# Routing stage of a mixture-of-experts layer: transposes ahead of products, row scales in pairs, a running sum by doubling, the tile map moved forward

## The chip, the cores and the metric

The kernel runs on one core of a Trainium2 chip. The metric is the device time of one execution in microseconds (us), taken as the median over runs. The core has five engines that run side by side and meet at semaphores: PE (TensorE, matrix products), DVE (VectorE), ACT (ScalarE), POOL (GpSimd) and SP (SyncE, which here only starts transfers). Transfers run on 16 DMA engines.

## The reference, cut to what matters

Two layers, each a recurrence ("cond") followed by a feed-forward part ("ffn"), added to x. The first ffn is attention and a mixture of experts over 1024 tokens of width 256; the change lies in its routing:

```
x = o @ wo + residual                       # end of attention
h = rmsnorm(x, ff_ln_w)
ht = h.reshape(-1, 256)                     # 1024 tokens
logits = ht @ gate_w                        # 8 experts
top_vals, top_idx = top_k(logits, 2)
gates = softmax(top_vals)
for e in range(8):
    we = sum(gates * (top_idx == e), axis=-1)
    ye = silu(ht @ w1[e]) * (ht @ w3[e]) @ w2[e]
    out = out + we[:, None] * ye
```

The second layer's recurrence and its ffn in 8-bit rounding follow; the work on their inputs runs beside the experts.

## The kernel before, in words

Every engine has one program, written out by hand; the order of the code is the order of the queue, and an instruction that waits holds back all that stands behind it on its engine. The stages around the change are these.

**Attention** ends with the output projection of the last four of the eight row tiles of 128 tokens (banks pb and pw). DVE adds the residual (`residual`, L1202, semaphore `x1a_done`, 3 and 4 for the last two pairs of tiles). Tiles 0 to 3 had theirs in the middle of attention, and their second norm is finished inside the attention steps.

**Second norm and gate.** For a tile ACT sums the squares (`squares_of_tile`, L838), POOL makes the reciprocal root of the sum (`rstd`, L1557 and L1558), DVE scales the rows into h2 (`second_norm`, L1212). SP stores each h2 tile to h2_dram. PE transposes the tile (2 instructions, L481), ACT copies the transpose out of the bank (`copy_h2T`, L862), PE multiplies it by gate_w (2 instructions of 8 columns, L485). `route(i)` holds a tile's transposes and products one behind the other.

**Choice of experts and slots.** DVE takes the two largest logits, makes 0/1 masks M1, M2 and their sum MK (L1241 to L1259). PE counts along the tokens of a tile (L529) and over each whole tile (L530). DVE adds up the tile totals one after the other (L1270, eight dependent additions of 128x8), rounds each expert's count up to whole tiles of 128 slots (L1272 to L1277), gives every token its two slots (L1279 to L1284), makes one-hot tables (L1295 to L1300), from which PE gets the token number of every slot (L536, bank pw, `ids_done`), and DVE writes these as integers (row_ids, L1309, `ids_ready`). The tile map (which expert each of the 23 tiles of slots belongs to, L1304 to L1307) and the end tile of each expert (L1311) also come from here; `tmap_ready` releases PE, ACT and SP.

`link(...)` lets an instruction raise a semaphore and DVE wait for it before the next one.

**Experts.** POOL gathers token rows for a tile of slots from h2_dram (L1640), four tiles ahead, then prepares the second layer's recurrence (L1572, L282), whose exponentials ACT makes (L717, L723) before its first silu (L932). PE transposes the rows (L575), multiplies by w1 and w3 (L583), and so on for 23 tiles. SP loads the experts' weights (`load_expert`; experts 1 and 2 start behind the stores of h2). POOL gathers the rows of the second ffn's weights (L1626) before the token rows.

**Last stage.** The second ffn, eight row tiles: products in `gate_up` (L659), transposes L670, products L680.

Of the kernel before, what the change touches and what calls it, by code (L numbers as in the profile page):

```python
# [13 lines left out]
P = 128  # L14
B, S, D = 4, 256, 256
TT = S // P
NT = B * TT
# [45 lines left out]
def build(nc, t, out):  # L63
    ctx = ExitStack()
    with ctx:
# [56 lines left out]
        def recurrence_buffers(base):  # L122
# [81 lines left out]
        lg, M1, M2, MK, tots, pos, prod = (rt[:, k, :] for k in range(7))  # L204
        m8 = rt[:, 7, :]
        i8 = rt[:, 8, :].bitcast(U32)
        car = rt[:, 9:11, :].rearrange("p a n -> p (a n)")[:, 0:(NT + 1) * NE]
# [36 lines left out]
            "hot_ready ids_done ids_ready identb_ready "  # L244
# [120 lines left out]
        def _(pe):  # L365
# [107 lines left out]
            def route(i):  # L473
# [8 lines left out]
                last.then_inc(s["h2T_done"], 1)  # L482
                pe.wait_ge(s["h2T_copied"], i + 1)
# [38 lines left out]
            pe.wait_ge(s["zeros_ready"], 1)  # L522
# [3 lines left out]
            for i in range(NT):  # L526
                route(i)
# [168 lines left out]
        def _(act):  # L696
# [168 lines left out]
            for i in range(4, NT):  # L865
                squares_of_tile(i)
            for i in range(1, NT):
                copy_h2T(i)
# [153 lines left out]
        def _(dve):  # L1022
# [187 lines left out]
            def second_norm(i):  # L1210
                dve.wait_ge(s["rstd2_ready"], i + 1)
# [48 lines left out]
            V.memset(car[:, 0:NE], 0.0).then_inc(s["d_ready"], 1)  # L1260
# [28 lines left out]
            link(V.tensor_copy(placef[:, :, :], place[:, :, :]))  # L1289
# [7 lines left out]
            for k in range(2):  # L1297
                V.tensor_tensor(hot_tile[:, k * NT:(k + 1) * NT], hot_tile[:, k * NT:(k + 1) * NT], over(token_id, MT), ALU.mult)
# [243 lines left out]
        def _(pool):  # L1542
# [197 lines left out]
```

## Time and profile before

| what | value |
|---|---|
| runs of the kernel before | 684.99, 678.54 and 681.04 us, median 681.04 |
| profiled execution | 683.2 us, of it the span of the trace 681.4 us |
| busy in the span | PE 507.7 us (75%), DVE 512.9 (75%), ACT 356.4 (52%), POOL 264.3 (39%) |
| mean granted TensorE clock | 0.916 of full speed |

The span runs from the first to the last instruction; the profiled execution's own time is 1.8 us more. No engine is busy throughout: the kernel is a line of stages with different limits, so what an edit is worth is read in its stage.

### The profile page before, as it was taken

Reading aid. Unit: us, or ns where it says so; the run is one execution under the profiler, and the core shown is the slowest. Engines: PE = TensorE matmul, PEld = TensorE weight load, DVE = VectorE, ACT = ScalarE, POOL = GpSimd, SP = SyncE. Lnnn points to the kernel's source line nnn. Section 1 sums busy time; section 2 is a strip of 40 time slices with the busy share of each in tenths; the row PEclk is TensorE's granted clock in tenths of the full one; section 3 lists DMA queues with packets and bytes.
Section 4 is the critical chain, followed back from the end, with each engine's and each line's share of the span. In section 5 each row is a group of like instructions: output and inputs, shape, how many; then the busy total and the mean of one; then the engine's idle time right before and its main releaser. Section 6 shows DMA issues by size and latency. Waiting matters only on the chain.

```text
span 681.4 us, 9298 instructions
## 1 busy us (share of the span) xinstructions
PE 507.7 (75%) x3018; PEld 345.2 (51%) x3018; DVE 512.9 (75%) x970; ACT 356.4 (52%) x758; POOL 264.3 (39%) x219
## 2 busy tenths in 40 slices
PE   2011296789999999997189989999999998046763
PEld 1001132468888788875145646566656665023442
DVE  4999875788888889872729779879798786379672
ACT  3236145677777778762034554635734554256452
POOL 3465024744444456415180683633350500530001
PEclk9999998799999999997579989999999999667685
DMA  8200003040000000004811942351443110210000
GB/s 269 99 0 0 0 1 123 5 158 1 2 1 1 1 1 25 9 1 141 257 39 28 313 85 44 120 148 29 173 144 117 25 23 16 79 53 8 16 16 24
DMA packets 28362, 44.23 MB, mean 65 GB/s; under 512 B 4795, under 2 KB 21435, under 8 KB 28059
## 3 DMA queue, kind: packets, MB, share of 16 engines
q1 hardware_dynamic: 20843, 31.43, 14.2%
q0 software_dynamic: 3072, 8.14, 5.0%
q10 hardware_dynamic: 4400, 4.06, 1.7%
q8 instruction: 25, 0.41, 0.3%
q14 instruction: 22, 0.18, 0.1%
HBM read 38.51 MB, written 5.12 MB: 64 GB/s over the span
## 4 chain that ended last, share of the span: by engine, by line
PE 52%; DVE 24%; ACT 8%; issue 7%; POOL 5%; DMA 1%; SPq 0%; ACTq 0%; DVEq 0%; POOLq 0%
PE pb L407 10%; PE pw L407 8%; PE pb L583 7%; PE sc L446 6%; PE sc L583 5%; PE po L407 4%; PE pt L457 3%; PE sc L659 2%; PE pb L659 2%; DVE areg L1077 2%; DVE areg L1063 2%; DVE areg L1061 2%; PE pt L592 1%; POOL breg L1626 1%; DVE areg L1410 1%
## 5 line engine op out<-in xcount | busy, mean ns | idle before, releaser
L583 PE MATMUL pb<-wreg,areg 128*128 x184 | 85.1, 606 | 0.8 <-ACT areg L898 0.8
L407 PE MATMUL pb<-areg,wreg 128*128 128x512 f16 x240 | 63.5, 404 | 14.3 <-ACT breg L800 9.0
L1598 POOL TENSOR_TENSOR breg<-breg,con 128x512 f32<-128x512 f32 x32 | 40.6, 1270 | 83.5 <-ACT breg L800 83.5
L407 PE MATMUL pw<-areg 128*128 128x256 f16 x406 | 59.5, 283 | 7.7 <-DVE areg L1418 7.7
L583 PE MATMUL sc<-wreg,areg 128*128 x184 | 63.2, 486 | 0.0
L808 ACT ACTIVATE breg<-breg,mx 128x128 f32<-128x128 f32 (+1 forms) x128 | 56.6, 445 | 1.6 <-DVE mx L1185 1.6
L583 PEld LDWEIGHTS pb<-wreg,areg 128*128 128x128 f32 x184 | 33.9, 195 | 36.3 <-issue 36.1
L407 PEld LDWEIGHTS pw<-areg 128*128 128x128 f16 x406 | 40.7, 101 | 18.3 <-DVE areg L1418 11.2
L446 PE MATMUL sc<-areg,breg 128*128 128x128 f32 (+1 forms) x256 | 47.7, 330 | 0.4 <-DVE mx L1185 0.4
L1640 POOL DMA_INDIRECT areg<-h_dram,row_ids x23 | 31.5, 1371 | 40.6 <-PE po L575 22.4
L1593 POOL TENSOR_TENSOR breg<-breg 128x512 f32<-128x512 f32 x32 | 44.4, 1388 | 4.5
L407 PEld LDWEIGHTS pb<-areg,wreg 128*128 128x128 f16 x240 | 22.7, 101 | 43.1 <-ACT breg L800 12.4
L817 ACT CAST breg<-pt 128x768 f16<-128x768 f32 x32 | 25.5, 798 | 34.9 <-PE pt L457 34.9
L446 PEld LDWEIGHTS sc<-areg,breg 128*128 128x128 f32 x256 | 38.8, 193 | 7.2 <-issue 1.5
L583 PEld LDWEIGHTS sc<-wreg,areg 128*128 128x128 f32 x184 | 33.2, 190 | 18.3
L1134 DVE TENSOR_TENSOR breg<-pb,con 128x512 f32<-128x512 f32 x40 | 27.6, 689 | 18.4 <-PE pb L407 15.9
L1185 DVE CUSTOM_DVE_ANT_0 breg<-sc,con 128x128 f32<-128x128 f32 (+1 forms) x128 | 38.1, 353 | 3.7 <-issue 1.2
L932 ACT ACTIVATE areg<-pb 128x512 f32<-128x512 f32 x23 | 13.8, 599 | 51.7 <-PE pb L583 51.6
L910 ACT ACTIVATE areg<-wreg 128x1792 f16 x23 | 39.6, 1724 | 0.0
L384 PE MATMUL sc<-con,areg 128*128 128x128 f32 x16 | 4.5, 435 | 46.0 <-DVE areg L1080 46.0
L1404 DVE TENSOR_TENSOR areg<-areg,pb 128x512 f32<-128x512 f32 x23 | 15.7, 683 | 29.5 <-ACT areg L932 20.6
L407 PE MATMUL po<-breg,areg 128*128 128x256 f16 (+1 forms) x384 | 36.9, 246 | 0.3 <-DVE areg L1196 0.3
(239 smaller groups left out, 1285.8 us busy)
## 6 DMA issues: line engine op xcount, KB each, us to landing
wreg<-in_L_ffn_w SPq DMA_DIRECT2D x24, 896.0 KB, 7.9
ys_dram<-areg ACTq DMA_DIRECT2D x23, 128.0 KB, 1.8
wreg<-in_L_ffn_wq SPq DMA_DIRECT2D x1, 2048.0 KB, 9.3
wreg<-in_L_ffn_wo SPq DMA_DIRECT2D x1, 2048.0 KB, 8.2
areg<-in_fside_BxSxS ACTq DMA_DIRECT2D x4, 256.0 KB, 5.7
x_in<-in_x SPq DMA_DIRECT2D x4, 256.0 KB, 5.4
h_dram<-areg SPq DMA_DIRECT2D x8, 128.0 KB, 1.7
out_dram<-areg SPq DMA_DIRECT2D x8, 128.0 KB, 1.7
```

The lines of the kernel that those rows point to most:

```text
L407: last = nc.tensor.matmul(bank, w(a), m(b), start=first and k == 0, stop=final and k == 2)
L446: last = nc.tensor.matmul(sc2[:, b, o:o + w], qr[:, buf, b * S + qb * P:b * S + (qb + 1) * P], kT[:, kv, pair * PAIR + b * S:pair * PAIR + ...
L583: last = nc.tensor.matmul(bank, xsT[:, parity, c * P:(c + 1) * P], wreg[:, bass.ds(base + (m * C + c) * FF + lo, w)], start=c == 0, stop=c ...
L659: last = nc.tensor.matmul(bank, qxT[:, c, :], w_fold[m][:, a, c, k * IH:(k + 1) * IH], start=c == 0 and a == 0, stop=c == C - 1 and a == 1)
L808: last = nc.scalar.activation(pr[:, parity, b, o:o + w], pr[:, parity, b, o:o + w], ACT.Exp, bias=mx[:, parity, k:k + 1], scale=-1.0, accu ...
L817: nc.scalar.copy(pT[:, parity, 0], pt2[:, :, 0:BLK]).then_inc(s["pThi_done"], 1)
L910: nc.scalar.activation(w2s[parity][0].rearrange("p c n -> p (c n)"), wreg[:, bass.ds((e % RING) * WEXP + 2 * C * FF, FC * D)], ACT.Copy, s ...
L1134: V.tensor_tensor(t1[:, parity, :].rearrange("p (b n) -> p b n", b=2), bank[:, :].rearrange("p (b n) -> p b n", b=2), rope_cos.rearrange(" ...
L1185: last = V.tensor_tensor_reduce(out=pr[:, parity, b, o:o + w], in0=sc2[:, b, o:o + w], in1=mask[:, o:o + w], scale=-SCALE, scalar=3e38, op ...
L1593: G.tensor_tensor(dst, t1[:, parity, :], t2[:, parity, :], ALU.add).then_inc(s["radd_done"], 1)
L1598: G.tensor_tensor(t2[:, parity, :].rearrange("p (b n) -> p b n", b=2), t2[:, parity, :].rearrange("p (b n) -> p b n", b=2), rope_sin.rearr ...
L1640: G.indirect_dma_start(out=xs[n % 4], out_offset=None, in_=h2_dram[:, :], in_offset=bass.IndirectOffsetOnAxis(ap=row_ids[:, n:n + 1], axis ...
```

## The change

- PE: `route` is cut in two. The transposes of tile i+1 now stand ahead of the products of tile i.
- ACT: behind the copy of tile 0 come the squares of tiles 4 and 5, then the copy of tile 1, then the squares of tiles 6 and 7. Before, all four squares came ahead of the copy of tile 1.
- POOL: the reciprocal roots are made for two tiles by one pair of instructions, and wait for the squares of both. POOL also clears a new buffer `prefix` at the start of the program.
- DVE: the running sum over tiles is made in three additions of 72 columns, each of the buffer and itself shifted by 8, 16 and 32 columns. The addition that gives `pos` moves ahead of the rounding of the counts, without a wait of its own. The two masked products and the two sums behind them lose the wait between them. The comparison of the tile map (cmp) moves behind the slots, its sum behind `placef`, and the map (tmi) and the ends (endi) ahead of hot_place. `tmap_ready` is raised behind identb, at the end.

```diff
-        lg, M1, M2, MK, tots, pos, prod = (rt[:, k, :] for k in range(7))
+        prefix = sb("prefix", [P, 4, NT * NE // 2 + (NT + 1) * NE])
+        sums_from = NT * NE // 2
+        lg, M1, M2, MK, prod2, pos, prod = (rt[:, k, :] for k in range(7))
-        car = rt[:, 9:11, :].rearrange("p a n -> p (a n)")[:, 0:(NT + 1) * NE]
+        car = prefix[:, 3, sums_from:]
...
-            for i in range(NT):
-                route(i)
+            for i in range(NT + 1):
+                if i < NT:
+                    route_transposes(i)
+                if i >= 1:
+                    route_products(i - 1)
...
             copy_h2T(0)
-            for i in range(4, NT):
-                squares_of_tile(i)
-            for i in range(1, NT):
+            squares_of_tile(4)
+            squares_of_tile(5)
+            copy_h2T(1)
+            squares_of_tile(6)
+            squares_of_tile(7)
+            for i in range(2, NT):
                 copy_h2T(i)
...
             def second_norm(i):
-                dve.wait_ge(s["rstd2_ready"], i + 1)
+                dve.wait_ge(s["rstd2_ready"], i // 2 + 1)
...
-            V.memset(car[:, 0:NE], 0.0).then_inc(s["d_ready"], 1)
+            dve.sem_inc(s["d_ready"], 1)
...
+            def before_by(x, n):
+                return x[:, sums_from - n:sums_from - n + (NT + 1) * NE]
+
+            dve.wait_ge(s["zeros_ready"], 2)
             dve.wait_ge(s["rank_done"], 1)
-            link(V.tensor_copy(tots, po[:, 256:256 + NT * NE]))
-            for i in range(NT):
-                link(V.tensor_tensor(car[:, (i + 1) * NE:(i + 2) * NE], car[:, i * NE:(i + 1) * NE], tots[:, i * NE:(i + 1) * NE], ALU.add))
+            link(V.tensor_copy(prefix[:, 0, sums_from + NE:], po[:, 256:256 + NT * NE]))
+            for k in range(3):
+                src = prefix[:, k]
+                link(V.tensor_tensor(before_by(prefix[:, k + 1], 0), before_by(src, 0), before_by(src, NE << k), ALU.add))
+
+            V.tensor_tensor(pos, po[:, 128:128 + NT * NE], car[:, 0:NT * NE], ALU.add)
...
-            link(V.tensor_tensor(pos, po[:, 128:128 + NT * NE], car[:, 0:NT * NE], ALU.add))
-            for k, M in enumerate((M1, M2)):
-                link(V.tensor_tensor(prod, pos, M, ALU.mult))
-                link(V.tensor_reduce(out=slotf[:, k, :], in_=te(prod), axis=AX.X, op=ALU.add))
-            link(V.tensor_copy(sloti[:, :, :], slotf[:, :, :]))
+            V.tensor_tensor(prod, pos, M1, ALU.mult)
+            link(V.tensor_tensor(prod2, pos, M2, ALU.mult))
+            V.tensor_reduce(out=slotf[:, 0, :], in_=te(prod), axis=AX.X, op=ALU.add)
+            link(V.tensor_reduce(out=slotf[:, 1, :], in_=te(prod2), axis=AX.X, op=ALU.add))
+            V.tensor_copy(sloti[:, :, :], slotf[:, :, :]).then_inc(s["dve_link"], 1)
...
+            dve.wait_ge(s["identb_ready"], 1)
+            dve.sem_inc(s["tmap_ready"], 1)
...
             def second_rstd(i):
-                pool.wait_ge(s["ssq2_ready"], i + 1)
-                rstd(i, 1, s["rstd2_ready"])
+                pool.wait_ge(s["ssq2_ready"], i + 2)
+                rstd(i, 2, s["rstd2_ready"])
...
-            for i in range(4, NT):
+            for i in range(4, NT, 2):
                 second_rstd(i)
```

The queue of PE at the start of the routing stage. In the names pb is the bank of the transposes, po that of the logits, and areg holds h2 and its transpose. Before:

```order
L481 MATMUL pb<-con,areg 128x128 [waits wo_step,h2_ready]
L481 MATMUL pb<-con,areg 128x128
L485 MATMUL po<-gate_w,areg 128x8 [waits h2T_copied]
L485 MATMUL po<-gate_w,areg 128x8
L481 MATMUL pb<-con,areg 128x128 [waits x1a_done,h2_ready]
```

And in the changed kernel, where the same code stands on L483 (transposes) and L490 (products):

```order
L483 MATMUL pb<-con,areg 128x128 [waits wo_step,h2_ready]
L483 MATMUL pb<-con,areg 128x128
L483 MATMUL pb<-con,areg 128x128 [waits x1a_done,h2_ready]
L483 MATMUL pb<-con,areg 128x128
L490 MATMUL po<-gate_w,areg 128x8 [waits h2T_copied]
L490 MATMUL po<-gate_w,areg 128x8
L483 MATMUL pb<-con,areg 128x128 [waits h2T_copied,h2_ready]
```

The products of tile 0 moved behind the transposes of tile 1, and with them behind the wait for `x1a_done`; so for every later pair.

The queue of DVE at the end of the slot tables (breg holds the one-hot tables, pw and row_ids the token numbers). Before:

```order
L1298 TENSOR_TENSOR breg<-breg,con 128x184
L1300 TENSOR_TENSOR breg<-con,placef 128x1024 x2
L1304 TENSOR_TENSOR cmp<-rt,con 128x184
L1306 TENSOR_REDUCE tmap<-cmp 128x23 [waits dve_link]
L1307 TENSOR_SCALAR tmi<-tmap 1x23 [waits dve_link]
L1309 CAST row_ids<-pw 128x23 [waits ids_done,dve_link]
L1311 TENSOR_SCALAR endi<-rt 1x8
L1313 CAST identb<-con 128x128
```

And in the changed kernel:

```order
L1302 CAST sloti<-slotf 128x16 [waits dve_link]
L1305 TENSOR_TENSOR cmp<-rt,con 128x184
L1310 TENSOR_SCALAR place<-sloti 128x16 [waits dve_link]
L1311 TENSOR_SCALAR place<-sloti 128x16
L1312 CAST placef<-place 128x32 [waits dve_link]
L1315 TENSOR_REDUCE tmap<-cmp 128x23 [waits cmp_ready]
L1322 TENSOR_TENSOR breg<-con,placef 128x368 [waits dve_link]
L1325 TENSOR_TENSOR breg<-breg,con 128x184 [waits dve_link]
L1325 TENSOR_TENSOR breg<-breg,con 128x184
L1327 TENSOR_SCALAR tmi<-tmap 1x23 [waits cmp_ready]
L1328 TENSOR_SCALAR endi<-rt 1x8
L1330 TENSOR_TENSOR breg<-con,placef 128x1024 x2
```

Four instructions (cmp, tmap, tmi, endi) that stood behind the last table, three of them ahead of row_ids, now stand ahead of it.

## Rows read from the trace of the kernel before

**Rows 1.** Windows by stage (busy of PE, PEld, DVE, ACT, POOL; clock, DMA)

```profile
309.80:324.80 15.00, 10.70 (x48) 7.92 (x48) 3.23 (x6) 4.46 (x16) 10.84 (x15) 0.65 0.58 180
324.80:339.90 15.10, 1.90 (x21) 1.51 (x20) 12.58 (x70) 0.22 (x1) 1.31 (x3) 0.50 0.90 271
```

**Rows 2.** Chain that ended last, in the routing stage (start us, us, what)

```profile
315.75 1.02 PE po L485 x4
316.78 0.53 PE pb L481 x2
...
317.33 0.38 ACT areg L862
...
317.76 1.02 PE po L485 x4
```

**Rows 3.** Timeline, same stage (start us, us, engine, line, operation)

```profile
310.44 0.68 DVE L1202 SCALAR_TENSOR_TENSOR x<-pw,x 128x512 f32<-128x512 f32 x1
...
312.14 0.19 ACT L838 ACTIVATION_READ_ACCUMULATOR areg<-x 128x1 f32 x1
...
313.98 0.79 PE L485 MATMUL po<-gate_w,areg 128*128 128x8 f32 x4 [0.46 <-ACT areg L862]
...
315.75 0.93 PEld L485 LDWEIGHTS po<-gate_w,areg 128*128 128x128 f32 x4 [0.86 <-ACT areg L862]
...
316.42 0.48 PEld L481 LDWEIGHTS pb<-con,areg 128*128 128x128 f32 x2
...
324.84 0.23 DVE L1241 COPY rt<-po 128x64 f32<-128x64 f32 x1 [8.58 <-PE po L485]
```

**Rows 4.** Window of PE (us, busy, instructions, granted clock, DMA share, GB/s)

```profile
314.00:315.00 1.00, 1.00 (x6) 0.63 0.26 92
```

**Rows 5.** POOL groups by shape, at the start, where two columns are made

```profile
L1558 POOL TENSOR_TENSOR ssq<-ssq,nhalf 128x2 f32<-128x2 f32 x2 | 2.0, 1010 | 0.2
L1557 POOL TENSOR_SCALAR ssq<-ssq 128x2 f32<-128x2 f32 x2 | 0.8, 420 | 10.7 <-ACT breg L758 10.7
```

**Rows 6.** Chain that ended last, in the slot stage (start us, us, what)

```profile
327.44 0.13 DVE rt L1257
...
329.46 0.18 DVE rt L1270
...
332.83 0.24 DVE rt L1282
...
338.02 0.27 DVE cmp L1304
...
338.31 0.36 DVE tmap L1306
...
338.69 0.18 DVE tmi L1307
...
338.89 0.19 DVE row_ids L1309
```

**Rows 7.** Transfers from issue to landing, us: token rows (L1640), then weight rows (L1626)

```profile
DMA to landing us min/median/max: 2.7/2.8/3.5
...
DMA to landing us min/median/max: 6.6/7.5/7.8
```

**Rows 8.** Window of PE; the last two columns are DMA share and GB/s

```profile
337.00:338.00 1.00, 0.33 (x8) 0.50 0.50 160
```

**Rows 9.** Timeline of the first tile of experts

```profile
339.85 0.97 POOL L1640 DMA_INDIRECT areg<-h_dram,row_ids  x1 [13.49 <-DVE row_ids L1309]
...
345.17 4.78 PE L583 MATMUL pb<-wreg,areg 128*128 x7
...
349.82 1.28 ACT L932 ACT_TABLE_LOAD   x1
```

**Rows 10.** Timeline of PE in the last stage, row tiles 2 and 6

```profile
614.50 2.43 PE L659 MATMUL sc<-x_in,areg 128*128 128x352 f16 x8 [3.31 <-ACT areg L969]
...
649.32 1.37 PE L659 MATMUL sc<-x_in,areg 128*128 128x352 f16 x8 [0.65 <-ACT areg L969]
```

More of the change, by code:

```diff
@@ L471, in weighted_values, with route_transposes @@
                 last.then_inc(s["av_done"], 1)
-            def route(i):
+            def route_transposes(i):
                 pe.wait_ge(s["h2_ready"], i + 1)
@@ L482, in route, with route_products @@
                 last.then_inc(s["h2T_done"], 1)
+            def route_products(i):
                 pe.wait_ge(s["h2T_copied"], i + 1)
@@ L1277, in _ @@
             link(V.tensor_scalar(ex8[:, 4, :], ex8[:, 3, :], float(P), None, ALU.mult))
-            link(V.tensor_tensor(pos, po[:, 128:128 + NT * NE], car[:, 0:NT * NE], ALU.add))
             link(V.tensor_tensor(te(pos), te(pos), ex8[:, 4:5, :].to_broadcast([P, NT, NE]), ALU.add))
-            for k, M in enumerate((M1, M2)):
-                link(V.tensor_tensor(prod, pos, M, ALU.mult))
-                link(V.tensor_reduce(out=slotf[:, k, :], in_=te(prod), axis=AX.X, op=ALU.add))
-            link(V.tensor_copy(sloti[:, :, :], slotf[:, :, :]))
+            V.tensor_tensor(prod, pos, M1, ALU.mult)
[3 more added lines that the diff above has]
+            V.tensor_copy(sloti[:, :, :], slotf[:, :, :]).then_inc(s["dve_link"], 1)
+            links[0] += 1
+            cmpv = cmp[:, :].rearrange("p (t e) -> p t e", e=NE)
+            V.tensor_tensor(cmpv, ex8[:, 2:3, :].to_broadcast([P, MT, NE]),
+                            iota_t.rearrange("p (t a) -> p t a", a=1).to_broadcast([P, MT, NE]), ALU.is_le).then_inc(s["cmp_ready"], 1)
+            dve.wait_ge(s["dve_link"], links[0])
             slots = sloti[:, :, :].rearrange("p k i -> p (k i)")
@@ L1288, in _ @@
             link(V.tensor_scalar(place[:, 1, :], slots, P - 1, None, ALU.bitwise_and))
-            link(V.tensor_copy(placef[:, :, :], place[:, :, :]))
+            V.tensor_copy(placef[:, :, :], place[:, :, :]).then_inc(s["dve_link"], 1)
+            links[0] += 1
+            dve.wait_ge(s["cmp_ready"], 1)
+            V.tensor_reduce(out=tmap[:, 0, :], in_=cmpv, axis=AX.X, op=ALU.add).then_inc(s["cmp_ready"], 1)
+            dve.wait_ge(s["dve_link"], links[0])
             def over(x, n):
@@ L1298, in _ @@
                 V.tensor_tensor(hot_tile[:, k * NT:(k + 1) * NT], hot_tile[:, k * NT:(k + 1) * NT], over(token_id, MT), ALU.mult)
+            dve.wait_ge(s["cmp_ready"], 2)
+            V.tensor_scalar(tmi[0:1, :], tmap[0:1, 0, :], float(NE - 1), None, ALU.min)
+            V.tensor_scalar(endi[0:1, :], ex8[0:1, 2, :], 1.0, None, ALU.add)
             for k in range(2):
@@ L1301, in _ @@
                                 over(placef[:, 1, k * NT:(k + 1) * NT], P), ALU.is_equal).then_inc(s["hot_ready"], 1)
-            cmpv = cmp[:, :].rearrange("p (t e) -> p t e", e=NE)
-            link(V.tensor_tensor(cmpv, ex8[:, 2:3, :].to_broadcast([P, MT, NE]),
-                                 iota_t.rearrange("p (t a) -> p t a", a=1).to_broadcast([P, MT, NE]), ALU.is_le))
-            link(V.tensor_reduce(out=tmap[:, 0, :], in_=cmpv, axis=AX.X, op=ALU.add))
-            link(V.tensor_scalar(tmi[0:1, :], tmap[0:1, 0, :], float(NE - 1), None, ALU.min))
             dve.wait_ge(s["ids_done"], 1)
             V.tensor_copy(row_ids[:, :], pw[:, 0:MT]).then_inc(s["ids_ready"], 1)
-            V.tensor_scalar(endi[0:1, :], ex8[0:1, 2, :], 1.0, None, ALU.add).then_inc(s["tmap_ready"], 1)
             V.tensor_copy(identb[:, :], ident).then_inc(s["identb_ready"], 1)
+            dve.wait_ge(s["identb_ready"], 1)
+            dve.sem_inc(s["tmap_ready"], 1)
             def round_e4m3(link, dst, v, g):
@@ L1552, in _ @@
             G.memset(zeros[:, :], 0.0).then_inc(s["zeros_ready"], 1)
+            G.memset(prefix[:, :, :], 0.0).then_inc(s["zeros_ready"], 1)
             link(G.memset(nhalf[:, :], -0.5))
@@ L1614, in step @@
                     rope_sum(KU + u, parity)
-                if H + LAG + 2 <= u < H + LAG + 6:
+                if u in (H + LAG + 2, H + LAG + 4):
                     second_rstd(u - H - LAG - 2)
```

4 lines of the change are left out of this document (2 added, 2 removed).

## The prediction

> **What bounds the kernel now.** I first read the busy shares: PE and DVE 75% each, so no engine is the bound and each stage needs its own reading. The windows show the two stages that the change touches: 15.0 us with PE busy for 10.7, then 15.1 us with DVE busy for 12.6 and PE for 1.9 [rows 1]. I then read the chain of work that ended last through both. In the first it goes round a ring between PE and ACT: products of a tile 1.02 us, transposes of the next tile 0.53, ACT's copy 0.38, and then the next products; the start of one product to the next is 2.01 us [rows 2]. Nothing of it overlaps: PE waits for ACT's copy, ACT for PE's transposes. DVE, which delivers the normalised tiles, is not late there; it waits 8.58 us for the last logits [rows 3]. In the second stage the chain is DVE alone, one small dependent instruction after the other, but for PE's two counting products and the token numbers, up to row_ids [rows 6]. Then POOL starts the gathers at 339.85 [rows 9], and all that follows (gathers, recurrence inputs, ACT's exponentials, the first silu) counts from there. So a microsecond taken from either stage should move everything behind it by a microsecond.
>
> **The ring of transposes and products.** With the transposes of tile i+1 ahead of the products of tile i, ACT's copy runs under products of 1.02 us, and 0.38 us plus some 0.08 of handing over fits. The period falls from 2.01 to at most 1.02 + 0.53 = 1.55 us. It can be less, since weight loads run ahead: the loads of a product and a transposition pair take 0.93 + 0.48 = 1.41 us [rows 3]. Between 1.41 and 1.55 I take 1.5.
>
> The start must be followed separately, since ACT's order changes. Tile 1's transposes wait for the residual, ready at 310.44 + 0.68 = 311.12 [rows 3], and so end at about 311.5; the products of tile 0 now stand behind them and end at about 312.1. That is later than now but holds nobody up: the next thing to be late is ACT. Its squares ended at 312.14 + 0.19 = 312.33 [rows 3]; with the copy of tile 1 (0.38) ahead of the last two they end at about 312.8, and the copy of tile 2 behind them at 313.2. So the products of tile 2 start at 313.2, where now they start at 313.98 [rows 3]: 0.8 us won. From there six products and four transposes remain. The clock fell from full to half within 314 to 315 (mean 0.63 [rows 4]), and the first products and transposes come ahead of that, as they do now: products of tile 2 and transposes of tile 4 0.9 us (half of 1.02 + 0.53, and a little), products of tile 3 0.95, three periods of 1.5, and the last products 1.02. Sum 7.4, end at 320.6. Now the last products end as DVE's copy begins, at 324.84 [rows 3]. Won: **4.2 us**. With periods of 1.41 it is 4.5, with 1.55 4.1. If only the copy is hidden, seven times 2.01 - 1.55 = 3.2, the low bound.
>
> **Row scales two at a time.** Two columns cost POOL 0.42 + 1.01 us at the start of the kernel [rows 5]. The squares of tiles 4 and 5 are done at about 311.5, the scales at 313.0, and DVE's rows of tile 4 (0.48 us) at 313.5; PE wants them at 313.7. Tiles 6 and 7: squares 312.8, scales 314.3, rows 314.8 and 315.3, wanted at 316.5 and later. So the pair hides behind the ring. Tile 4 has only 0.2 us of cover; were it 1 us late, the ring would end 0.8 later, which I keep as a bound. The products of tile 3 are queued on PE behind that wait, and ACT's copies of tiles 4 and up behind them. In attention the pairs stand at every other step of the two that POOL served before, and POOL is busy only 39% of the span. SP's stores of h2 wait for the same rows, in the order they have now; the last is ready about 1 us earlier, and the loads of experts 1 and 2 behind them start so much earlier.
>
> **DVE's running sum.** Eight additions at a pitch of 0.18 + 0.02 = 0.20 [rows 6] are 1.61 us. The three that replace them are 72 columns wide; the nearest row is 64 columns, 0.24 + 0.02 = 0.26 [rows 6], so 0.78. Won 0.83. The copy of the totals ahead of them keeps its size. The buffer that POOL clears is cleared where POOL has nothing to do yet: nothing. The cleared head of car (one memset) stood behind the masks, beside PE's counting: nothing.
>
> **Waits between independent operations.** An instruction of 64 columns with no wait behind it costs 0.13 us [rows 6] where a waited one costs 0.26. That is 0.12 for pos and 0.11 each for the pair of products and the pair of sums: **0.34**.
>
> **Tile map moved forward.** Behind the last one-hot table now come cmp 0.27, 0.02, tmap 0.36, 0.02, tmi 0.18, 0.02: 0.87 us, then row_ids at 338.89 [rows 6]. With them gone, row_ids waits for PE's eight products, which start with the table's end and take some 0.45 us: 0.4 won. But the four instructions now stand ahead of the tables, on the chain. They no longer wait for each other. cmp and tmap are as wide as each other and cost 0.27 with no wait behind them; each fills a wait (behind sloti and placef) that cost some 0.12, so 0.15 each. tmi and endi I take at half of 0.18 each. Sum 0.48. The bounds are 0.3 (if most hides in the waits) and 0.8 (each at its full duration). So this edit **costs 0.1 us**, between a win of 0.1 and a loss of 0.4. tmap_ready comes about 0.3 us later relative to row_ids; PE needs it only with the gathered rows, over 2.7 us later [rows 7]: nothing.
>
> **Sum.** 4.2 + 0.83 + 0.34 - 0.1 = 5.3 us. The profiled execution took 683.2 us; it would take 677.9. It lay 2.2 us above the median of 681.04, so I forecast **675.7 us**.
>
> **What could eat it: the gathers meet the weights.** POOL's first gather would start at 339.85 - 5.3 = 334.5. The weight stream of experts 1 and 2 saturates the DMA engines until about 337.5 [rows 8], some 1 us less in the changed kernel. Gathers in that stream landed 7.5 us after issue, gathers behind it 2.8 [rows 7]. The Trainium skill speaks against the change here (DMA: Bandwidth & Descriptors, "Issuing engines are not separate DMA queues"): transfers run on the same 16 DMA engines and interleave, whichever engine started them. The trace agrees, by the 7.5 us. At the full price the first gather lands 4.7 us late. PE has a cover of 1.15 us there, since its first tile ends at 349.95 and ACT's table load only at 351.10 [rows 9]; so 3.5 us would be lost, and 1.8 are left: 679.2 us. Against it: the stream ends 2 us after the first issue, so the gather cannot be held for long. I expect under 1.15 us, which is hidden.
>
> **Rival: the clock stays full.** PE is busier in the new ring: no gaps of 0.46 us. If the clock doesn't fall at 314, five periods of about 0.8 replace those of 1.5, less what the row scales let through (the last rows at 315.3): the ring ends at about 317.7, 2.9 us earlier. That gives 675.7 - 2.9 = 672.8 us. For it: the gaps go. Against it: PE was busy for 10.7 of the stage's 15.0 us [rows 1] and for the whole of the microsecond in which the clock fell [rows 4], and it stayed at half to the stage's end. The Trainium skill (TensorE: Matmul & The Clock Gate, "Part 4: PE-mode transpose") says that the full clock does not engage for transposes; by it the forecast stands.
>
> **Rival: slower, by the clock of the last stage.** The same eight products of a half take 1.37 us at full clock and 2.43 at half [rows 10], 2.1 us a row tile for both halves. Which tiles get the full clock is not fixed by the program: tile 6 had it, tile 2, with the same work, not. Everything behind the routing now comes 5.3 us earlier, so the tiles may meet the clock otherwise. Two tiles lost cost 4.2, and the change still gains 1.1; from the third on (6.4) it is slower: 682.1 us. The runs of before, 678.5 to 685.0, show that such shifts come without any change.
>
> **Rival: the ring gains little.** If the row scales or the copy of tile 2 come late and the periods are 1.55, with the low bound 3.2 and 0.8 less: 2.4 + 1.1 = 3.5, so 677.5 us.
>
> **How the numbers follow.** The forecast, 674 to 677: 0.52. Clock kept, 671 to 674: 0.23. Little gain, 677 to 678.5: 0.10. Gathers late, 679: 0.08. Slower, 682 and more: 0.07. A measurement of this kernel can't tell less than about 1%, 6.8 us, from no change; the line is 674.2. The clock's case lies beyond it, and some 0.3 of the forecast's, since medians scatter by over a microsecond: 0.23 + 0.15 = 0.38 faster. Slower by 1% needs six tiles lost (12.6 less 5.3), or three and the gathers late: 0.04, and not less, since medians scatter. The rest is 0.58. The range leaves out half of the slow case and the best of the clock's with such scatter: 670.5 to 680.5.
>
> **What would show it.** In the profile after: products and transposes of the ring back to back, some 1.4 to 1.55 us a tile at half clock, and DVE's copy of the logits about 4.2 us earlier (320.6); three additions of 0.26; row_ids about 0.45 us behind the last table; the first gather near 334.5 and PE's first transposes of token rows near 337.4. A copy of the logits near 317.7 shows the clock kept; PE's first token rows at 339 or later show the gathers late, if ACT's table load comes first no more. What would make me wrong most: a period of the ring that is set by something I took as hidden, such as ACT's copy or the two-column scales.

## The result, and the profile after

| what | value |
|---|---|
| kernel before, runs beside those of the change | median 684.66 us (678.54 to 687.63, 22 runs) |
| changed kernel | median 678.76 us (675.42 to 681.34, 22 runs) |
| ratio | 0.9916, 95% interval 0.9897 to 0.9935: 5.7 us faster (4.5 to 7.0) |
| forecast | 5.3 us faster: 675.7 us from the 681.04 of the first three runs, range 670.5 to 680.5 |
| profiled execution | 679.51 us, span 677.7 (before 683.2 and 681.4) |

Ratios are taken without the runs that fell in a slower state, so they need not be the quotient of the medians (here 5.9 us apart). The gain is nearly the forecast's, but not in the way that the forecast gave. The windows of the two stages in the changed kernel (busy of PE, PEld, DVE, ACT and POOL, granted clock, DMA share, GB/s), the same stages as [rows 1]:

```profile
309.40:318.60 9.20, 7.92 (x48) 7.33 (x48) 3.05 (x6) 4.38 (x16) 5.66 (x8) 0.74 0.40 109
318.60:332.50 13.90, 1.90 (x21) 1.51 (x20) 11.31 (x64) 0.22 (x1) 4.62 (x5) 0.50 1.06 317
```

The first shrank from 15.0 us to 9.2 with the same 48 PE instructions, the second from 15.1 to 13.9 with six DVE instructions fewer. Together they shrank by 7.0 us and the profiled span only by 3.7, so something was given back behind them. The chain of work that ended last, from the ring to PE's first token rows (start us, us, what; L483 transposes, L490 products, L870 ACT's copy, L1287 the running sum, L1334 row_ids, L583 transposes of token rows, L591 the experts' first products):

```profile
312.44 0.36 ACT areg L870
312.80 0.04 issue
312.84 0.61 PE po L490 x4
313.45 0.27 PE pb L483 x2
313.73 0.50 PE po L490 x4
314.23 0.52 PE pb L483 x2
314.75 0.65 PE po L490 x4
315.40 0.52 PE pb L483 x2
315.92 0.65 PE po L490 x4
316.58 0.52 PE pb L483 x2
317.10 1.51 PE po L490 x8
...
323.28 0.23 DVE prefix L1287
...
323.55 0.23 DVE prefix L1287
...
331.57 0.19 DVE row_ids L1334
...
332.53 5.60 DMA areg<-h_dram,row_ids
...
338.17 0.70 PE po L583 x2
...
339.66 6.10 PE pb L591 x8
```

Three things are to be seen. ACT's copy, 0.38 us in each round of [rows 2], has left the chain after 312.8: PE follows PE. The pitch of the ring at half clock is 0.65 + 0.52 = 1.17 us, where it was 2.01. And a gather stands in the chain with 5.60 us, where gathers of token rows landed after 2.8 [rows 7]. row_ids comes 338.89 - 331.57 = 7.32 us earlier than in [rows 6], PE's first token rows only 342.68 - 338.17 = 4.51 earlier. The windows of PE around the clock's fall (us, busy of the five, clock, DMA share, GB/s):

```profile
312.00:313.00 1.00, 0.82 (x8) 0.58 (x7) 0.64 (x2) 1.00 (x6) 0.63 (x3) 1.00 0.00 0
313.00:314.00 1.00, 1.00 (x10) 1.00 (x11) 0.42 (x2) 0.31 (x2) 0.79 (x1) 0.88 0.27 96
314.00:315.00 1.00, 1.00 (x7) 1.00 (x7) 0.70 (x2) 0.35 (x2) 0.99 (x1) 0.50 0.48 166
316.00:317.00 1.00, 1.00 (x7) 1.00 (x7) 0.00 (x0) 0.33 (x1) 0.70 (x1) 0.50 0.96 98
```

The clock fell from full (2.4 GHz) to half (1.2 GHz) close to the forecast's moment, though PE was busy through the whole of the microsecond in which it fell and of those behind it.

**The measure used from here on.** Runs of one kernel scatter by 6 to 9 us, so each kernel is compared by marks in its trace: T0 is PE's first transpose of tile 0 in the ring; "ring" is from T0 to DVE's copy of the logits; "slots" from there to row_ids; "landing" from POOL's first gather to PE's first transposes of token rows; tile 1 and tile 22 are the starts of the up products of those tiles of slots, from T0. All in us.

| kernel | ring | slots | landing | tile 1 | tile 22 |
|---|---|---|---|---|---|
| before | 14.98 | 14.05 | 2.83 | 42.88 | 253.02 |
| changed | 9.15 | 12.93 | 5.64 | 38.89 | 249.21 |
| ring_only | 8.84 | 14.16 | 4.92 | 39.28 | 248.94 |
| slots_only | 14.93 | 13.52 | 2.82 | 42.46 | 253.10 |
| after_late2 | 9.10 | 12.94 | 2.76 | 35.89 | 246.72 |
| before_late2 | 14.80 | 14.79 | 2.86 | 43.44 | 253.40 |
| single_scales | 9.22 | 12.96 | 5.89 | 39.03 | 249.32 |
| squares_first | 9.42 | 12.89 | 5.91 | 39.15 | 249.45 |
| serial_ring | 14.31 | 12.89 | 2.84 | 41.67 | 251.11 |
| ring_late2 | 9.07 | 14.03 | 2.84 | 36.96 | 248.31 |
| early | 9.03 | 13.99 | 2.90 | 36.36 | 245.71 |
| early_warm | 9.40 | 13.60 | 2.82 | 35.99 | 246.31 |
| late2_again | 8.96 | 12.94 | 2.78 | 35.80 | 246.56 |
| after_again | 8.97 | 13.07 | 5.55 | 38.91 | 249.25 |

Each row is one execution, so the scatter of a column matters. The slot stage of the changed kernel repeats within 0.2 us. The ring that eight of these kernels share took 8.84 to 9.40 us, and the clock orders it: where the granted clock falls later, more of the ring runs at full clock. By the mean clock of the microsecond in which it fell (0.88 in 313 to 314 of the changed kernel, 0.78 in 314 to 315 of ring_only, 0.79 in 312 to 313 of early_warm) the fall came 4.3, 4.9 and 4.0 us behind T0, and the rings took 9.15, 8.84 and 9.40. Tile 1 also holds the first up products of the experts, which took 5.3 to 6.5 us according to how far into them the clock rose again.

### The profile page after: what moved, and what is told of

Its sections match the earlier page's. It is cut to its first block, busy times and chain, and to the rows that moved or that the text cites. A ratio compares the mean times of both kernels' runs of the same rounds, so it can differ in the third digit from the quotient of the medians.

```text
span 677.7 us, 9286 instructions
## 1 busy us (share of the span) xinstructions
PE 505.3 (75%) x3018; PEld 345.5 (51%) x3018; DVE 511.8 (76%) x964; ACT 356.6 (53%) x758; POOL 261.6 (39%) x212
## 4 chain that ended last, share of the span: by engine, by line
PE 52%; DVE 23%; issue 10%; ACT 7%; POOL 3%; DMA 2%; SPq 0%; DVEq 0%; ACTq 0%; POOLq 0%; PEldq 0%
PE pb L409 10%; PE pw L409 8%; PE pb L591 8%; PE sc L448 5%; PE sc L591 5%; PE po L409 4%; PE pt L459 3%; PE sc L667 2%; PE pb L667 2%; DVE areg L1088 2%; DVE areg L1074 2%; DVE areg L1072 2%; PE pt L600 1%; POOL breg L1652 1%; DVE areg L1435 1%
## 5 line engine op out<-in xcount | busy, mean ns | idle before, releaser
L591 PE MATMUL pb<-wreg,areg 128*128 x184 | 85.6, 609 | 0.8 <-ACT areg L909 0.8
L409 PE MATMUL pw<-areg 128*128 128x256 f16 x406 | 57.9, 277 | 7.3 <-DVE areg L1443 7.3
L591 PE MATMUL sc<-wreg,areg 128*128 x184 | 63.2, 486 | 0.0
L591 PEld LDWEIGHTS pb<-wreg,areg 128*128 128x128 f32 x184 | 34.4, 197 | 36.4 <-issue 35.9
L591 PEld LDWEIGHTS sc<-wreg,areg 128*128 128x128 f32 x184 | 33.2, 190 | 18.3
```

The lines of the kernel that those rows point to most:

```text
L409: last = nc.tensor.matmul(bank, w(a), m(b), start=first and k == 0, stop=final and k == 2)
L591: last = nc.tensor.matmul(bank, xsT[:, parity, c * P:(c + 1) * P], wreg[:, bass.ds(base + (m * C + c) * FF + lo, w)], start=c == 0, stop=c ...
```

## The experiments

### The two halves of the change, apart

**ring_only** is the changed kernel with DVE's slot stage as it was before:

```diff
+            link(V.tensor_copy(tots, po[:, 256:256 + NT * NE]))
+            for i in range(NT):
+                link(V.tensor_tensor(car[:, (i + 1) * NE:(i + 2) * NE], car[:, i * NE:(i + 1) * NE], tots[:, i * NE:(i + 1) * NE], ALU.add))
...
```

(and the other lines of DVE's slot stage, the tile map behind the tables among them). **slots_only** is the reverse: the kernel before, with DVE's slot stage of the change.

> The changed kernel with the old order of the slot stage: only PE's order, ACT's order and the paired row scales are changed. Theory 1 (the end of the weight stream decides when the first token rows land): row_ids come about 6.2 us earlier than in the kernel before (5.8 from the ring), the first gather is issued near 333.7 and its rows still reach PE near 338.2, as in the full change; the gain is that of the full change, 5.7 us within the measurement (ratio about 0.992). Rival (the parts add up and the gathers lose a fixed time in the stream): 1.1 us less than the full change, PE's first token rows near 339.3, ratio about 0.993 to 0.994.

> The kernel before with only the slot stage of the change: running sum by doubling, dropped waits, tile map moved. Theory: row_ids 1.1 us earlier, the ring as before; the first gather is then issued at about 338.7, behind the weight stream (end 337.5), and lands after the usual 2.8 us, so PE's first token rows are 1.1 us earlier and the kernel 1.1 us faster (ratio 0.998), hard to tell from nothing in the times but plain in the trace. Rival: the four instructions moved ahead of the tables cost as much as the sum saves, row_ids within 0.3 us of before, no gain.

Measured: ring_only 672.95 us, ratio to the kernel before 0.9866 (0.9813 to 0.9919); slots_only 682.38, ratio 0.9992 (0.9951 to 1.0032). In ring_only PE's first token rows start at 338.56, nearer to the theory's 338.2 than to the rival's 339.3; its ratio is better than either had it, which the last stage explains in part (below). The ring alone reaches tile 22 as early as the whole change (248.94 and 249.21). The slot edits shortened their stage by 14.16 - 12.93 = 1.23 us in the changed kernel and by 0.53 in slots_only, and moved tile 22 in neither. row_ids of slots_only came 0.58 us earlier from T0, where 1.1 was expected. In slots_only 0.64 us of it went in a gap ahead of DVE's cast of the chosen indices, 0.83 us from the start of the last search to the cast where the kernel before has 0.19, with nothing in the trace to explain it (two rows of its timeline; the bracket is the idle time, put down to the search itself):

```profile
327.18 0.16 DVE L1248 FIND_INDEX8 rt<-rt 128x8 uint32<-128x8 f32 x1
328.01 0.17 DVE L1257 CAST rt<-rt 128x16 f32<-128x16 uint32 x1 [0.68 <-DVE rt L1248]
```

before_late2 has the same gap (330.70 to 331.66), which is its long slot stage. Without it slots_only's stage would be 12.9 us. For the changed kernel most of the reason is in the landing: counted from T0, ring_only issues its first gather 0.9 us later, but its landing is 0.7 us shorter, so PE's first token rows are only 0.2 apart (28.88 and 28.68 us behind T0). The rows land when the weight stream lets them, so the landing takes most of what the slots win. The 0.4 us that are left at tile 1 go with the 0.65 us that all kernels with the slot edits lose between tiles 9 and 10 (see Open).

### The weights of expert 2 behind the first gathers

**after_late2** and **before_late2** change SP's order in the changed kernel and in the kernel before:

```diff
             load_expert(sp, 1)
-            load_expert(sp, 2)
...
             for e in range(NE):
+                if e == 2:
+                    sp.wait_ge(s_xs[3], 16)
+                    load_expert(sp, 2)
```

s_xs[3] is raised by the fourth gather's landing; the load now stands in SP's loop over the experts.

> The changed kernel, with expert 2's weights (half of the stream) requested only when the first four gathers have landed. Theory 1 (the gathers land late because the stream still runs): the stream ends near 327, the first token rows land 2.8 us after issue instead of 5.6, PE's first transposes of them at about 335.4 instead of 338.2, and the kernel gains 2 to 2.8 us on the full change: ratio to the kernel before about 0.988. Rival 1 (the late start of the experts comes from POOL's issuing and not from the stream): no change against the full change. Rival 2: expert 2's weights then come too late or collide with other gathers, and PE waits for them later: the gain is lost again.

> The kernel before, with the same delay of expert 2's weights. Theory 1: in the kernel before the gathers are issued behind the end of the stream, so nothing is gained: first token rows 2.8 us behind issue as before, ratio 1.000 within 0.002. Rival (late weights are better for another reason, such as POOL's weight rows landing earlier): a gain of 1 us or more here too.

Measured: after_late2 674.15 us, ratio 0.9892 (0.9828 to 0.9957); before_late2 686.98, ratio 1.0003 (0.9959 to 1.0046). In the traces the edit takes the landing from 5.64 to 2.76 us in the changed kernel and moves tile 1 by 3.0 and tile 22 by 2.5; in the kernel before it moves nothing forward (2.86, 253.40). The same window in the two traces, first the changed kernel:

```profile
335.00:336.00 1.00, 0.00 (x0) 0.00 (x0) 0.00 (x0) 0.00 (x0) 0.92 (x1) 0.50 1.09 351
```

and then after_late2:

```profile
335.00:336.00 1.00, 0.25 (x2) 0.00 (x0) 0.00 (x0) 0.37 (x1) 0.70 (x2) 0.50 0.44 86
```

DMA share 1.09 against 0.44, and PE and ACT at work on the first rows in the second only. By queue, the changed kernel moves 315 packets of weights and 7 of the gathers in 335 to 336, and 94 and 70 in the microsecond after. So the weight stream caused the late landing, and it was paid nearly in full at tile 1 (3.0 us, of which 0.2 are the clock in the first up products, 6.08 and 5.86 us). The two kernels were set side by side once more, to see whether the total shows it:

> The changed kernel with late weights of expert 2 again, beside the changed kernel itself. Theory: 2.5 us faster than the changed kernel up to the last tile of experts, as in its first profile; the median of the whole 2 to 4 us lower, the last stage scattering with the clock.

> The changed kernel itself, on the chip of the three others. Theory: ratio 0.992 to the kernel before, as recorded, and the token rows late behind the weight stream as in its profile (landing 4.5 to 5.6 us behind issue).

late2_again 677.69 us, ratio 0.9913 (0.9871 to 0.9956); after_again 678.49, ratio 0.9941 (0.9908 to 0.9973). The traces repeat (tile 22 at 246.56 and 249.25, 2.7 us apart); the totals, 0.8 us apart where 2 to 4 were expected, don't separate the two.

### Inside the ring

**serial_ring** undoes PE's order alone, **squares_first** ACT's alone, **single_scales** POOL's pairs alone:

```diff
-            for i in range(NT + 1):
-                if i < NT:
-                    route_transposes(i)
-                if i >= 1:
-                    route_products(i - 1)
+            for i in range(NT):
+                route_transposes(i)
+                route_products(i)
```

```diff
             copy_h2T(0)
-            squares_of_tile(4)
-            squares_of_tile(5)
-            copy_h2T(1)
-            squares_of_tile(6)
-            squares_of_tile(7)
-            for i in range(2, NT):
+            for i in range(4, NT):
+                squares_of_tile(i)
+            for i in range(1, NT):
                 copy_h2T(i)
```

```diff
-                dve.wait_ge(s["rstd2_ready"], i // 2 + 1)
+                dve.wait_ge(s["rstd2_ready"], i + 1)
...
-                pool.wait_ge(s["ssq2_ready"], i + 2)
-                rstd(i, 2, s["rstd2_ready"])
+                pool.wait_ge(s["ssq2_ready"], i + 1)
+                rstd(i, 1, s["rstd2_ready"])
...
```

> The changed kernel with transposes and products of a tile one behind the other again on PE; ACT's order and the pairs stay. Theory: the order on PE is what the ring gained, and the period goes back to 2.0 us: ring 14 to 14.5 us against 14.98 before and 9.15 after. Rival: a part of the 5.8 us came from the pairs, ring near 12.

> The changed kernel with ACT's old order: all four squares ahead of the copy of tile 1. Theory: the copies of tiles 1 and 2, and with them the products of tile 2, come 0.7 us later, all else is the same: ring 9.8 us. Rival: the later squares are hidden, ring 9.15 us.

> The changed kernel with the row scales made one tile at a time again. In the changed kernel PE's transposes of tiles 4 to 7 start 3.8, 4.6, 5.8 and 6.9 us behind those of tile 0, and single scales had these rows ready at 2.8, 4.0, 5.2 and 6.4 us. Theory: the pairs give nothing, the ring (first transposes of tile 0 to DVE's copy of the logits) stays at 9.15 us within 0.2. Rival: single scales hold PE back now that the ring is fast, 9.6 us or more.

One run each: 684.49, 679.45 and 679.69 us, beside one of the kernel before with 679.47, so these totals tell nothing; only the traces do. The ring took 14.31, 9.42 and 9.22 us, against 9.15. PE's order is worth 14.31 - 9.15 = 5.2 us of the 5.8; ACT's order with the pairs 0.7 when PE is serial, but only 0.27 and 0.07 one at a time on top of PE's order. The 0.07 is less than the shared ring scatters by. The 0.27 is not told by the clock, which fell 4.3 us behind T0 as in the changed kernel, but it is one trace, and lies between the two expectations (9.8 and 9.15). The chain of squares_first shows why ACT's order matters little:

```profile
311.92 0.19 ACT areg L846
312.11 0.27 ACT areg L870
312.38 0.04 issue
312.42 0.61 PE po L490 x4
313.04 0.27 PE pb L483 x2
313.31 0.35 PE po L490 x4
```

The four squares end at 312.11 and two copies follow at once, both of their transposes being long done. PE's products of tile 1 start late, at 312.42, but those of tile 2 follow after 0.89 us, and the delay is nearly made up. The chain of serial_ring repeats the old round at a pitch of 2.01 us:

```profile
318.07 0.38 ACT areg L868
...
318.49 1.02 PE po L490 x4
319.52 0.53 PE pb L483 x2
...
320.07 0.38 ACT areg L868
```

serial_ring also bears out the stream: its gathers go out behind it (landing 2.84), and there the slot edits count in full. PE's first token rows come 31.00 us behind T0, before 32.82: 1.8 us earlier, 0.7 from the ring and 1.2 from the slots. At tile 1 only 1.2 are left, since its first up products took 6.54 us and those of the kernel before 5.79; that tile 22 is again 1.9 earlier comes about by later steps that scatter (see Open).

**ring_late2** is ring_only with the late load of after_late2:

> The ring changes without the slot changes, and with expert 2's weights behind the first four gathers. Theory: with the weight stream out of the way the slot changes count in full: compared with the full change and the same late weights (first token rows on PE 25.76 us behind the first transposes of tile 0), 1.2 us later, 27.0 us, the landing 2.8 us behind the issue. Rival: the slot changes are worth nothing in any surrounding: 25.8 us.

676.40 us in one run. Its landing is 2.84, and between it and after_late2 the slot edits are worth 26.90 - 25.76 = 1.14 us at PE's first token rows (27.0 - 25.8 was expected), 1.07 at tile 1. With the stream out of the way they count; behind it they don't.

### Using what the landing leaves free

**early** adds to after_late2: POOL's first recurrence work for the second layer goes ahead of the token gathers, and ACT's two exponentials on it right behind the gates:

```diff
+            recurrence_inputs(1, 0, 0)
...
-            exponentials_at = {0: 0, 5: 1, 8: 2, 14: 3}
+            exponentials_at = {5: 1, 8: 2, 14: 3}
```

**early_warm** adds to that seven matrix products whose results nobody reads, to raise the clock before the token rows come, four behind the counting products and three behind `ids_done`:

```diff
+            def busy(n):
+                for _ in range(n):
+                    nc.tensor.matmul(sc2[:, 0, :], ones, con[:, o:o + 2 * S], start=True, stop=True)
...
+            busy(4)
...
+            busy(3)
```

> The changed kernel, expert 2's weights behind the first four gathers, and the second layer's recurrence inputs of batch 0 (three POOL instructions, ACT's two exponentials) moved ahead of the wait for the token numbers, where POOL and ACT idle. Theory: with the stream out of the way the first silu waits for the exponentials and the table load (341.75 and 343.05 in the run with late weights alone), so it would come when PE's first products end: the silu 0.9 us earlier and the experts 0.5 to 1 us earlier, tile 1 at about 35.3 us behind the first transposes instead of 35.9. Rival: POOL's work beside DVE's small instructions slows the slot stage (12.93 us) by as much.

> As the run before it, with seven products of constants (128x512, nobody reads them) that keep PE busy: four behind the counting products, three behind the token numbers. Theory: TensorE's clock is at full when the token rows come, so the first tile's products take 3.6 us instead of 6 and tile 1 starts 2 to 2.4 us earlier than in the run before it, about 33 us behind the first transposes. Rival: the clock does not rise, or falls before the rows come: the four products at half clock then end behind the one-hot tables and cost up to 1 us.

early: 673.5 us, ratio 0.9882 (0.9821 to 0.9944). early_warm: 673.94, 0.9867 (0.9809 to 0.9925). early lost 1.05 us in the slots (13.99 against 12.94, both counted from DVE's copy of the logits) and won 1.0 by tile 22. Tile 1 came at 36.36, not at the 35.3 of the theory and later than without the edit (35.89): the rival held there. What it wins it wins behind tile 1: 0.5 from tile 1 to 2, where ACT is no longer late (see the account of the cover below), and 0.9 between tiles 5 and 7, where the steps scatter over all these kernels, so that this part is not shown to be the edit's. The loss in the slots has its rows in the timeline of early: POOL's work runs beside DVE's small instructions, and several of these take longer, two of them 0.50 and 0.45 us where their kind takes 0.17. Others beside the same POOL instruction keep their 0.17 (L1296):

```profile
324.65 1.51 POOL L1607 TENSOR_SCALAR areg<-ratio 128x512 f32<-128x512 f32 x1
324.80 0.50 DVE L1295 CAST rt<-exi 128x8 f32<-128x8 int32 x1
325.33 0.17 DVE L1296 TENSOR_TENSOR_SCAN rt<-con,rt 128x8 f32<-128x8 f32 x1
...
325.74 0.45 DVE L1298 TENSOR_SCALAR rt<-rt 128x8 f32<-128x8 f32 x1
```

early_warm's products did raise the clock, but it did not last. Its windows:

```profile
330.00:333.00 3.00, 2.21 (x20) 1.33 (x21) 1.41 (x3) 0.00 (x0) 0.47 (x1) 1.00 0.00 0
333.00:336.00 3.00, 1.63 (x5) 0.39 (x3) 0.00 (x0) 0.10 (x1) 2.39 (x3) 1.00 0.24 67
336.00:339.00 3.00, 2.40 (x3) 1.17 (x4) 0.00 (x0) 1.55 (x2) 2.67 (x4) 0.58 0.43 108
```

The clock was full when the rows came (PE's first transposes of them at 335.35), and fell near 336.5, just as the up products of tile 0 began (336.60): they took 5.31 us, in early 5.34, and not the 3.6 hoped for. Tile 1 came 0.4 us earlier than in early, at 35.99 where 33 was expected, tile 22 0.6 later. This much work, put there, did not carry the clock over the wait.

## Why the prediction was right, and where two errors met

**The time itself.** The forecast of 675.7 stood on a median of 681.04 from three runs; beside the changed kernel the kernel before had 684.66, 3.6 us more. So 678.76 lies in the stated range, but outside the 674 to 677 that had 0.52, while the difference, 5.7, is near the 5.3. Both have to be judged by their terms.

**The ring's start: right.** Products of tile 2 were forecast for 313.2 and started at 312.84, with T0 0.37 us earlier. The clock fell about where forecast.

**The products of the ring: the term that was mis-sized.** The ring gave 14.98 - 9.15 = 5.8 us, not 4.2. The prediction took 1.5 us for a period at half clock, between 1.41 and 1.55; measured 1.17, and the whole three periods 3.63 us for 4.5. The products of tile 3, across the fall of the clock, took 0.50 us for 0.95, and the last ones 0.75 for 1.02. These make 0.87 + 0.45 + 0.27 = 1.6 us, and all have one root: the sizes of the products were taken from a ring in which they wait for ACT. The step that failed is "the loads of a product and a transposition pair take 0.93 + 0.48 = 1.41 us", used as the lower bound. The rows of one round in the changed kernel's timeline show that it bounds nothing:

```profile
315.04 0.48 PEld L483 LDWEIGHTS pb<-con,areg 128*128 128x128 f32 x2
315.25 0.67 PE L483 MATMUL pb<-con,areg 128*128 128x128 f32 x2
315.50 0.98 PEld L490 LDWEIGHTS po<-gate_w,areg 128*128 128x128 f32 x4
315.71 0.86 PE L490 MATMUL po<-gate_w,areg 128*128 128x8 f32 x4
```

From one pair of loads to the next (315.04 to 316.22) are 1.18 us, in which loads with recorded times of 0.48 + 0.98 = 1.46 us stand: the records overlap, as those of the matrix products do. The products took 1.02 us in the old ring and in serial_ring, where PE waits for ACT ahead of them, and add 0.65 to a round in which it doesn't; that their first load then runs beside the transposes is how I read these rows.

**The clock stays full: it did not.** PE was busy for all of 313 to 317, and the clock fell within 313 to 314 and stayed at 0.50. This was given 0.23. In all 14 traces it fell 4.0 to 4.9 us behind T0, in the old ring with its waits (4.4 in the kernel before, 4.1 in serial_ring) as in the new one, so the waits that the change removed did not decide it. What did is not shown. Until it fell the transposes ran at the full clock too: two of them took 0.27 us at 313.45 and 0.52 behind the fall.

**Row scales in pairs: nothing, as forecast** (single_scales 9.22 against 9.15). The risk at tile 4 did not come: POOL's pair of instructions for tiles 4 and 5 took 0.19 and 0.70 us there, where [rows 5] had 0.42 and 1.01.

**Running sum and unlinked instructions: right.** Three additions at a pitch of 0.27, as forecast (0.26). The slot stage shrank by 1.12, forecast 0.83 + 0.34 - 0.1 = 1.07. The tile map cost 0.1 on the chain, as forecast: these rows of the chain hold its four instructions, cmp (L1305), tmap (L1315), tmi and endi:

```profile
326.70 0.26 DVE cmp L1305
...
327.33 0.25 DVE tmap L1315
...
328.67 0.07 DVE tmi L1327
328.75 0.07 DVE endi L1328
```

From sloti to place it is now 0.43 us and was 0.21; from placef to the second table (L1325, before L1298) 0.91 and was 0.79, since the first table is 0.09 shorter on the chain behind tmap (0.46 for 0.55); tmi and endi add 0.15. That is 0.49, forecast 0.48, and row_ids comes 0.39 earlier behind the last table: 0.1.

**The gathers meet the weights: a rival at 0.08, and it happened in part.** It was forecast as hidden by "a cover of 1.15 us, since its first tile ends at 349.95 and ACT's table load only at 351.10". That step failed twice. The gather was held not for less than 1.15 but for 2.8 us, partly because the ring won more, so that it went out at 332.53 and not at 334.5, into more of the stream. (The price of 4.7 us came from gathers of weight rows, the only ones in the stream; for the token rows the experiments measured 2.8.) And the cover was nearly none. The up products of tile 1 write the bank that ACT's first silu and DVE's product behind it read (pb), so a late table load can hold PE there, but not from the end of tile 0's up products on: the gate products of tile 0 come between. These are PE's gate products of tile 0 and up products of tile 1, in the kernel before and then in the changed one:

```profile
350.00 2.75 PE L583 MATMUL sc<-wreg,areg 128*128 x8
352.74 3.69 PE L583 MATMUL pb<-wreg,areg 128*128 x8
```

```profile
345.80 2.75 PE L591 MATMUL sc<-wreg,areg 128*128 x8
348.38 3.60 PE L591 MATMUL pb<-wreg,areg 128*128 x8
```

They stand 2.74 us apart before and 2.58 in the changed kernel, whose table load (342.51 to 343.79) is out of the way. So in the kernel before PE did wait for the chain of silu and product (the product ends at 352.43), but only for 0.16 us: that was the cover at tile 1, where 1.15 was taken. One tile on there was 0.5 more: the step from tile 1 to tile 2 took 11.24 us before, 10.73 in the changed kernel, and 10.73 in early too, where the landing is on time and the table load out of the way. It is also why the late load of expert 2 wins 3.0 us at tile 1 and 2.5 at tile 22: after_late2 has 11.24.

The rule cited in the prediction (the Trainium skill, DMA: Bandwidth & Descriptors, "Issuing engines are not separate DMA queues") is borne out, and the experiments add its size here: 2.8 us for a gather issued some 4 us ahead of the stream's end.

**The sum.** To tile 1 from T0: 5.8 (ring) + 1.1 (slots) - 2.8 (landing) = 4.1, measured 42.88 - 38.89 = 4.0. Forecast 4.2 + 1.1 - 0 = 5.3. A ring 1.6 better makes up for more than half of a landing 2.8 worse. The total that came out, 5.7 us by the ratio, is larger than what the traces show at tile 22 (3.8 from T0) and at the end of the profiled pair (3.7). The other 2 us are put to no edit; the last stage, which differs by more than that from execution to execution, is where they can lie. That the total lies so near the forecast is luck.

**The clock of the last stage: the mechanism is there, the sign open.** From tile 22 to the end, by the spans, the same code took these times (us):

| before | changed | after_again | ring_only | ring_late2 | after_late2 | late2_again | before_late2 |
|---|---|---|---|---|---|---|---|
| 118.5 | 119.0 | 115.8 | 112.8 | 112.9 | 114.4 | 118.4 | 118.5 |

The same products of row tiles 3 and 4 (counted from 0) in the timeline of the changed kernel, and then of ring_only:

```profile
618.69 2.53 PE L667 MATMUL sc<-x_in,areg 128*128 128x352 f16 x8 [2.60 <-ACT areg L980]
...
628.93 2.53 PE L667 MATMUL sc<-x_in,areg 128*128 128x352 f16 x8 [2.24 <-ACT areg L980]
```

```profile
617.92 2.16 PE L667 MATMUL sc<-x_in,areg 128*128 128x352 f16 x8 [2.72 <-ACT areg L980]
...
627.11 1.37 PE L667 MATMUL sc<-x_in,areg 128*128 128x352 f16 x8 [2.24 <-ACT areg L980]
```

Which row tile gets 1.37 us and which 2.53 differs between kernels whose code is equal there, and the length differs for one and the same kernel between executions (119.0 and 115.8; 114.4 and 118.4). Within one kernel it is worth 3 to 4 us, over all of them 6 and more (serial_ring has 120.3), as much as the whole change. So the slower case that the prediction built on it was a real possibility. Whether ring_only, at 0.9866 some 3.4 us below the changed kernel's 0.9916, has a better pattern as a rule or drew better executions is open: the intervals (0.9813 to 0.9919 and 0.9897 to 0.9935) overlap, but ring_late2, the other kernel with the new ring and the old slot stage, has the same short last stage (112.9), with row tiles 3 and 4 at 2.10 and 1.37 us.

**Open.** All kernels with the slot edits lose 0.65 us between tiles 9 and 10 (11.18 against 10.53), slots_only too, in which nothing else there differs. All other steps from tile to tile agree within 0.06 us in all 14 traces but for three (1 to 2, explained above, 5 to 6 with 12.99 to 15.13, and 6 to 7 with 9.29 to 10.00), so this is not scatter. Most of it is a gap in DVE's own queue ahead of one expert instruction, 0.72 us in slots_only where the kernel before has 0.28 at the same instruction (serial_ring has 0.42), like the one ahead of the cast in slots_only and before_late2. Both come and go as other code is edited; their cause was not found. The first is why slots_only, 0.42 us ahead at tile 1, is not ahead at tile 22.

**The best version.** The changed kernel with the late load of expert 2 reaches tile 22 2.5 to 2.7 us earlier than the change (early 3.5). The totals (0.9892, 0.9913, 0.9882 against 0.9916 and 0.9941) lie the same way but overlap; only the trace resolves it.

## What to carry to other kernels

When a chain ahead of a transfer is shortened, look at what fills the DMA engines at the new time of issue: here 0.7 of the 0.9 us by which the slot edits brought the first gather forward went into the landing, until one weight load was moved behind four gathers. A cover is worth only as long as the engine that waits for the late thing would have waited anyway: PE's wait behind ACT's table load was 0.16 us, not the 1.15 by which ACT was late. And the recorded times of weight loads do not add up to a bound, since they overlap: here only the pitch of a stretch in which PE never waited gave the period.

## What the runs showed of the hardware

- Two transposes of 128x128 and two products of 8 columns, fp32, took 1.17 us a round at half clock with PE never idle. At full clock a round took 0.62 (0.35 + 0.27 in squares_first), and 0.89 where the products had waited for ACT's copy.
- TensorE's granted clock fell to 0.50 and stayed there while PE was busy for 1.00 of every microsecond with such small products. In early_warm, with seven further products between the waits, it was 1.00 in 330 to 336, and fell again within 336 to 339 (0.58), while PE had idled for part of 334 to 337.
- While a POOL tensor instruction of 128x512 ran beside DVE, two DVE instructions of 8 columns took 0.45 and 0.50 us in place of 0.17 and two others kept their 0.17 (early); the slot stage was 1.05 us longer.
- A gather issued some 4 us before the end of a weight stream with a DMA share of 1.03 to 1.09 reached PE after 5.6 us; behind the stream the same gather took 2.8.
- DVE instructions that need not wait for each other cost 0.07 (8 or 23 columns) to 0.15 (64 columns) each on the chain, wider ones (184 columns) 0.25; those of 8 to 72 columns that wait 0.20 to 0.27.
